# Graph attention heads: a fourth of ten source blocks taken from TensorE and ScalarE to VectorE, and the next head's rows turned and fetched earlier

## The reference, cut to what matters

```python
z = (x @ W).reshape(N, num_heads, head_dim)
el = jnp.sum(z * attn_l, axis=-1)
er = jnp.sum(z * attn_r, axis=-1)
e = jax.nn.leaky_relu(el[src] + er[dst], NEG_SLOPE)
m = jax.ops.segment_max(e, dst, num_segments=N)
ex = jnp.exp(e - m[dst])
denom = jax.ops.segment_sum(ex, dst, num_segments=N)
alpha = ex / denom[dst]
out = jax.ops.segment_sum(alpha[:, :, None] * z[src], dst, num_segments=N)
out = out + z + bias
```

## Time and profile before

| | |
|---|---|
| time, median of 3 runs | 3422.15 us (3420.96 to 3429.84) |
| profiled execution | 3426.71 us, its span 3425.0 us |
| mean granted TensorE clock | 0.916 of full |
| PE, PEld busy | 85%, 63% of the span |
| DVE, ACT, POOL busy | 56%, 33%, 4% |
| heads of g0, first to last exponent matmul and sums | about 360 to 831 us |
| heads of g1 | about 976 to 1446 us |

### The profile page before, as it was taken

One profiled execution on the slowest core, in us unless ns is written; L12 is line 12 of the kernel. 1 busy time (PEld: TensorE's weight loads), 2 busy tenths in 40 slices (PEclk: granted clock), 3 DMA queues, 4 the chain that ended last, 5 costly groups with the idle time before them and its releaser, 6 DMA issues.

```text
span 3425.0 us, 45464 instructions
## 1 busy us (share of the span) xinstructions
PE 2909.4 (85%) x14613; PEld 2142.6 (63%) x14614; DVE 1915.6 (56%) x3661; ACT 1137.0 (33%) x1827; POOL 132.9 (4%) x189
## 2 busy tenths in 40 slices
PE   6876699998949999896969679889995998896994
PEld 4543588887538888763657434468884565465772
DVE  7755899984679999557331134476641333532113
ACT  0111588875247777522014211121110220211110
POOL 0000000000000000000001110000000000000112
PEclk9888799999979999998979889979997999897995
DMA  1011111101011111100125542122213110023434
GB/s 67 0 35 42 45 47 61 49 37 50 2 67 46 45 55 48 50 0 25 58 78 190 189 126 72 45 75 82 74 30 135 44 40 21 32 79 112 165 136 146
DMA packets 80976, 231.30 MB, mean 68 GB/s; under 512 B 14037, under 2 KB 26783, under 8 KB 77985
## 3 DMA queue, kind: packets, MB, share of 16 engines
q1 hardware_dynamic: 58161, 166.83, 13.5%
q0 software_dynamic: 16304, 47.67, 4.7%
q10 hardware_dynamic: 6400, 15.36, 1.3%
HBM read 177.60 MB, written 54.94 MB: 68 GB/s over the span
## 4 chain that ended last, share of the span: by engine, by line
PE 39%; DVE 6%; DMA 5%; issue 2%; ACT 1%; POOL 0%; SPq 0%; ACTq 0%; DVEq 0%; POOLq 0%
PE psum L998 17%; PE psum L917 10%; PE psum L1123 4%; PE psum L1132 4%; DMA arena<-y_rows,arena 2%; DVE arena L1559 1%; DMA y_rows<-arena 1%; DMA arena<-xn_rows,arena 1%; PE psum L1071 1%; DMA arena<-raw 1%; DVE arena L1681 1%; DVE arena L1867 1%; PE psum L1105 1%; PE psum L1110 1%; PE psum L907 0%
## 5 line engine op out<-in xcount | busy, mean ns | idle before, releaser
L998 PE MATMUL psum<-arena 125*125 125x256 f32 (+3 forms) x2400 | 630.0, 422 | 46.2 <-DVE arena L1695 46.2
L917 PE MATMUL psum<-arena 128*125 128x384 f32 (+1 forms) x1840 | 662.6, 519 | 7.3 <-ACT arena L1235 7.3
L1028 PEld LDWEIGHTS psum<-arena 125*125 125x125 f32 x4800 | 579.7, 190 | 66.1 <-DVE arena L1692 16.0
L998 PEld LDWEIGHTS psum<-arena 125*125 125x125 f32 x2400 | 449.5, 189 | 215.7 <-DVE arena L1695 40.0
L1028 PE MATMUL psum<-arena 125*125 (+1 forms) x4800 | 566.0, 271 | 13.6 <-DVE arena L1692 13.6
L917 PEld LDWEIGHTS psum<-arena 128*125 128x125 f32 x1840 | 344.9, 190 | 298.7 <-issue 115.1
L1018 PE MATMUL psum<-arena,spread 126*125 126x313 f32 (+1 forms) x1344 | 438.4, 450 | 31.8 <-DMA arena<-r_rows 18.2
L1692 DVE SCALAR_TENSOR_TENSOR arena<-arena,edge_counts 125x625 f32<-125x625 f32 x480 | 383.1, 807 | 86.0 <-ACT arena L1320 85.3
L1625 DVE CUSTOM_DVE_ANT_0 arena<-arena,no_edge_bias 125x1250 bf16<-125x1250 f32 x270 | 393.3, 1457 | 32.8 <-DMA arena<-el_rows 27.3
L1307 ACT ACTIVATE arena<-arena,el 125x625 f32<-125x625 f32 x480 | 386.5, 806 | 38.2 <-DMA arena<-el_rows 38.2
L1320 ACT ACTIVATE arena<-psum,el 125x625 f32<-125x625 f32 x336 | 262.6, 781 | 204.9 <-PE psum L1018 185.1
(11 more groups left out here) (212 smaller groups left out, 2399.2 us busy)
## 6 DMA issues: line engine op xcount, KB each, us to landing
arena<-el_rows SPq DMA_DIRECT2D x51, 610.4 KB
arena<-in_L_ffn_W SPq DMA_DIRECT2D x16, 1152.0 KB, 9.2
y_rows<-arena SPq DMA_DIRECT2D x47, 384.0 KB, 2.4
arena<-r_rows SPq DMA_DIRECT2D x24, 610.4 KB
arena<-in_L_w SPq DMA_DIRECT2D x16, 768.0 KB, 6.3
arena<-in_L_gnn_W SPq DMA_DIRECT2D x4, 3072.0 KB, 14.6
raw<-arena POOLq DMA_DIRECT2D x40, 250.0 KB, 2.9
arena<-raw SPq DMA_DIRECT2D x10, 1000.0 KB
```

The lines of the kernel that those rows point to most:

```text
L917: ins = e.matmul(bank[0:P, 0:w], L.xt[u][:, k, :], L.w_sb[:, k, at:at + w], start=(k == 0), stop=(k == L.KT - 1))
L998: ins = e.matmul(banks[2 + 2 * (j % 2) + c][0:P, 0:w], Ph[half][:, s, d * P:(d + 1) * P], (L.zh[u] if L.spill else L.z)[:, s, at:at + w], ...
L1028: ins = e.matmul(banks[2 + half][0:P, d * 65:(d + 1) * 65], Ph[half][:, s, d * P:(d + 1) * P], L.z[:, s, h, :], start=(s == 0), stop=(s == ...
```

## The change

`ADD_AT` gets a fourth block, s = 5, so eight of a head's twenty blocks have their exponent from VectorE. The addition there is another one: instead of relu block + rb2 it is max(rb1 + el8, rb2), with a second broadcast row rb1. So the relu's of all eight blocks are dropped (`relu` returns), as are the exponent matmuls of blocks 5 and 15. SP writes all 20 rows of r_rows instead of 10 and loads rb1 and rb2. The load of the el row of head h + 2 moves from between the two halves' r2 rows to right behind the write, ahead of the wait for it. From head 1 on, the next head's rows are turned at block 4 and copied at block 5; head 0 keeps 11 and 12. ScalarE's code gets heads 0 and 1 out of its loop. Buffers in SBUF move to make room for rb1: the head buffers start at HEADS_AT, 40 columns above S_AT, and some buffers of the next layer's start move with them.

```diff
-ADD_AT = [3, 7, 9]
+ADD_AT = [3, 5, 7, 9]
...
+def rectified(j):
+
+    return j - of_vector(j)
...
-            rb_in=[16 * n * own for n in of_dma], relued=2 * T * heads * self.batched, t_ready=TURNS * heads * self.batched,
-            added=ADDS * heads * self.batched, rb2_in=[16 * n * self.batched for n in of],
+            rb_in=[16 * n * own for n in of_dma], relued=TURNS * heads * self.batched, t_ready=TURNS * heads * self.batched,
+            added=ADDS * heads * self.batched, rb2_in=[32 * n * self.batched for n in of],
...
+        ROWS_FROM = Z_AT + T * 12 * 65
+        HEADS_AT = ROWS_FROM + 2 * N
...
-            at = S_AT
+            at = HEADS_AT if L.batched else S_AT
...
+                L.rb1 = [carve(ROWS_FROM + u * N, P, N) for u in range(2)]
...
-        TURN_EARLY, ROWS_EARLY = 11, 12
+        TURN_EARLY, ROWS_EARLY = 4, 5
+        TURN_FIRST, ROWS_FIRST = 11, 12
...
-                e.dma_start(r_rows[h, T:2 * T, :], L.rt[u][T:2 * T, :]).then_inc(L.r_out[u], 16)
+                e.dma_start(r_rows[h, :, :], L.rt[u]).then_inc(L.r_out[u], 16)
+                if more:
+                    load_el(h + 2, u)
...
-                e.dma_start(L.rb2[u], over(r_rows[h, T:2 * T, :].rearrange("t p -> (t p)"))).then_inc(L.rb2_in[u], 16)
+                for rows, r in ((L.rb1, 0), (L.rb2, 1)):
+                    e.dma_start(rows[u], over(r_rows[h, r * T:(r + 1) * T, :].rearrange("t p -> (t p)"))).then_inc(L.rb2_in[u], 16)
...
-                    if half == 0 and more:
-                        load_el(h + 2, u)
...
-                    if j == TURN_EARLY and not last:
+                    if j == (TURN_FIRST if first else TURN_EARLY) and not last:
                         turn_r(h + 1, 1 - u)
...
+                if s in ADD_AT:
+                    return
...
-                    if j == ROWS_EARLY and not last:
+                    if j == (ROWS_FIRST if isinstance(h, int) and h == 0 else ROWS_EARLY) and not last:
                         rows(h + 1, 1 - u)
...
-                with e.Fori(0, L.H // 2 - 1) as i:
+                batched_head(0, 0, 0, False)
+                batched_head(1, 1, 0, False)
+                with e.Fori(1, L.H // 2 - 1) as i:
...
-                    e.wait_ge(L.rb2_in[u], L.since["rb2_in"][u] + 16 * (i + 1))
-                e.wait_ge(L.relued, L.since["relued"] + 2 * T * h + j + 1)
+                    e.wait_ge(L.rb2_in[u], L.since["rb2_in"][u] + 32 * (i + 1))
                 e.wait_ge(L.p_ready, L.since["p_ready"] + 2 * T * h + j + 1)
                 apart(e)
-                e.tensor_tensor(L.ex[j % 4], L.r2[half][0:P, s % 3, :], L.rb2[u][:, half * HALF:(half + 1) * HALF], ALU.add).then_inc(L.added, 1)
+                cols = slice(half * HALF, (half + 1) * HALF)
+                e.scalar_tensor_tensor(out=L.ex[j % 4], in0=L.rb1[u][:, cols], scalar=L.el8[:, s, bass.ds(h, 1)], in1=L.rb2[u][:, cols],
+                                       op0=ALU.add, op1=ALU.max).then_inc(L.added, 1)
```

More of the change, by code:

```diff
@@ L351, in graph_transformer @@
             else:
+                if L.inner is not None:
+                    at = HEADS_AT + 2 * N
                 L.xin = [carve(at + u * L.K, P, L.K) for u in range(2)]
@@ L356, in graph_transformer @@
                 at += 2 * L.K
-                L.xbias = carve(Z_AT + T * 12 * 65 if L.inner is not None else at, P, L.K)
+                L.xbias = carve(HEADS_AT + 2 * L.F if L.inner is not None else at, P, L.K)
                 at += L.K
@@ L364, in graph_transformer @@
                 L.sjunk = carve(at, P, 384).bitcast(BF16)
-            vectors_at = MADE_AT if L.spill else S_AT - 2 * L.F
+            vectors_at = MADE_AT if L.spill else HEADS_AT if L.inner is not None else S_AT - 2 * L.F
             L.al_b = [carve(vectors_at + u * L.F, P, L.F).rearrange("p (h d) -> p h d", h=L.H) for u in range(2)]
-            at = S_AT
+            at = HEADS_AT if L.batched else S_AT
             if L.H > 1:
@@ L643, in rows_of @@
                 def rows_of(h, u, i, more):
-                    e.wait_ge(L.relued, L.since["relued"] + 2 * T * (h - 1))
+                    e.wait_ge(L.relued, L.since["relued"] + TURNS * (h - 1))
                     apart(e)
@@ L1013, in exponents @@
                     e.wait_ge(L.r2_in[half], L.since["r2_in"][half] + 48 * (h + 1))
-                e.wait_ge(L.relued, L.since["relued"] + 2 * T * h + j + 1)
+                e.wait_ge(L.relued, L.since["relued"] + TURNS * h + rectified(j) + 1)
                 e.wait_ge(L.e_ready, L.since["e_ready"] + 2 * T * h + j + 1)
```

## The result

The changed kernel takes 3493.85 us (median of 4 runs, 3487.96 to 3497.49), the kernel before 3425.99 (4 runs, the three known ones and one more). The ratio is 1.019, 95% interval 1.017 to 1.022: slower by 1.9%, 68 us, where 37 were forecast. The profiled execution took 3494.81 us with a span of 3493.1, 68.1 us more than that of before.

A forecast was written before the change was run, and what follows sets the result against it. PE paced steady heads at 37.2 us, DVE close behind. Per layer 10.0 + 1.9 + 8.7 + 2.0 - 4.0 = +18.6 us, +37.2 for two, taking the median from 3422.2 to 3459.4, forecast 3460 us; range 3438 to 3484.

The forecast's parts named there:

- The direction and its first reason: Whole kernel slower, chance 0.90; in steady heads DVE becomes the limit, 38.2 us against PE's 37.2 before.
- the 0.2 us of disturbance: Steady heads: block 2 or 4 may reach DVE late, 0.2 us per head (bounds 0 and 0.5), making 38.4.
- The start: Start of each layer's heads: small r2 rows queue behind the el row and rb1 broadcasts, +8.7 us per layer.
- the small rows are not held up: Rival for the layer's start and h = 1: the 8.7 and 2.0 us vanish, result 3439 us; chance 0.10.
- Head 0: First head of each layer: two more additions and a dearer kind on DVE's path, +1.9 us per layer.
- Can DVE really run without waits?: Steady heads: PE idles about 3 us, then 3.4 us at half rate costs it 1.7: 36.8, under 38.2.
- PE's clock falls in every head for long: Rival for steady heads: half rate lasts some 17 us, PE needs 43.6 us; 3554 us in all; clock chance 0.10.
- case of every third head: Variant of the clock rival: the long half-rate stretch comes in every third head, some 3490 us in all.
- base of 35.1 us of PE work: PE per steady head: 37.2 us less 2.1 for the dropped exponent matmuls of blocks 5 and 15.
- the end of g0: Last max_end to last p_free in layer g0: 78.9 us, or 80.6 with 3.4 us at half rate; -4.0 taken.
- The start of h = 1: Second head: PE idles 4 us for late rows, likely falls to half rate; DVE waits, +2.0 us per layer.
- ACT's saved relu's and the earlier turn: Steady heads: eight relu's dropped at 0.8 us and loads moved to the fourth and fifth block gain nothing.

The follow-up runs named there:

- the first experiment: Changed kernel with the el row of head h + 2 loaded between the halves' small r2 rows again, as before the change: 3480.6 us, ratio 1.016.
- the first two experiments: Changed kernel with the el row's load back in its old place, 3480.6 us; changed kernel with small r2 rows first in heads 0 and 1, 3471.4 us.
- the last experiment: Kernel before, with four more unused VectorE additions of 625 columns per head in heads 1 to 9: 3492.5 us, ratio 1.020.
- experiment 8: Not a run's number: 8 counts waits in "the last experiment 8 of 9 waits"; that run is the kernel before with four more VectorE additions per head, 3492.5 us.

## Why the prediction was right or wrong, point by point

**The direction and its first reason held.** "So after the change DVE sets the pace, at 38.2 us against 37.2": a head without a fall is 38.27 us in both layers, without the 0.2 us of disturbance that were added to it. The addition costs the 0.78 us read from L1681, start to start:

```profile
478.12 0.86 DVE L1790 SCALAR_TENSOR_TENSOR arena<-arena,el 125x625 f32<-125x625 f32 x1
478.90 0.80 DVE L1708 SCALAR_TENSOR_TENSOR arena<-arena,edge_counts 125x625 f32<-125x625 f32 x1
```

The run without the scalar shows the 0.06 us that the row had over the old form. The Trainium skill's fixed part plus elements (VectorE: DVE Perf Modes, TRN2 errata) has no place for it; the measurement decides.

**The start held.** +9.1 and +8.9 us for the 8.7 worked out, and two runs with another order in the queue (DVE idle 22.0, 18.1, 7.3 us) show the cause. The rival "the small rows are not held up" is out. **Head 0** is exact.

**What failed: "Can DVE really run without waits?", in the price of the clock's fall.** The wait of PE was foreseen, at about 3 us; it is 2.1 to 2.2 us. The step then took the one case of the earlier trace rows, 3.4 us at half rate, as the size of every fall, and priced it at nothing, because 1.7 us fit under PE's slack. In the changed kernel the falls in steady heads last 6.8 us (head of 39.7 us), 10.2 (41.3) and 13.7 (42.9 to 43.0), in the first experiment 20.5 (46.2). The excess over 38.3 is half the length of the fall less PE's wait of 2.2 us: 6.8 / 2 - 2.2 = 1.2 for 1.5 measured, 13.7 / 2 - 2.2 = 4.7 for 4.6, 20.5 / 2 - 2.2 = 8.1 for 8.0. That is the mechanism of the rival "PE's clock falls in every head for long", which had 0.10. Its case of every third head is what came, and its 3490 us is near the 3494 measured, but in part by luck: it took every fall at 17 us and left the start of head 1 and the ends as they were forecast. Its base of 35.1 us of PE work was also low, since PE is busy for 36.07 us in head 2: with 35.1 a fall of 13.7 us would make a head of 42.0 us, with 36.07 one of 42.9, as measured. Heads 2 to 9 were +35.5 us instead of +18.8, and the end of g0, forecast with at most 3.4 us at half rate, had 13.7 and gave +1.6 instead of -4 us. Filler on PE takes all of this away, and load on DVE alone brings such falls about in the kernel before. The trace of before could not give the price: behind such a wait, with PE busy from then on, it has one fall per layer (413.1 us in g0, 1027.5 in g1), and both last 3.4 us. Its longer low stretches lie where PE waits again and again or has little to do.

**What failed second: "The start of h = 1", a term mis-sized.** PE's wait of 4 us was 6.3 and 6.7, and "likely falls to half rate" was priced at 3.2 us more of PE work. In g0 the clock was low for 34.1 us, 30 of them from the moment when PE could start: +14.3 us instead of +2.6, and +5.6 in g1, where the clock was low for 12 us from that moment on. The prediction saw only the late rows as the reason to wait. With the rows early PE waits 4.9 us at block 1 for DVE, which lags after head 0's twenty maxima. It did so before as well (2.94 us); two more additions in head 0 make it longer. With the small rows first it is 4.9 and 4.2 us with eight of the new additions, 2.8 and 3.4 with six.

**The end** came out as worked where the clock held: 78.9 us in g1.

**ACT's saved relu's and the earlier turn are worth nothing**, as said: with three blocks, where six blocks have no relu, a steady head takes the 37.2 us of before, and the earlier turn alone has a ratio of 1.000.

**What stays open.** Why a wait of the same 2.2 us is followed by a fall in one head and not in another, and what sets the length of a fall. What the runs show: in the changed kernel and the first two experiments 18 of 32 waits of 1.9 to 2.2 us had a fall behind them and none of 16 waits of about 1.0 us; with half the filler none of the waits of 1.0 to 1.1 us had one; in the last experiment 8 of 9 waits of 1.7 to 1.85 us had one.

## What to carry to other kernels

When a change makes another engine the limit, the loss is not the difference of the two periods alone: look where TensorE then waits. One fall of its clock in the trace does not give the length of the next: here 3.4 us before became 6.8 to 20.5 us, so such a term needs a wide range, or a run. If the wait can't be avoided, a few matmuls on constants in its place hold the clock, and a run with them tells the clock's share from the work's. In a queue, put the small transfer that an engine waits for ahead of the broadcasts; that alone made the kernel before 0.3% faster, and both versions that beat the kernel before have it.

## What the runs showed of the hardware that was not expected

- A fall of the granted clock to 0.50 after one wait of about 2 us lasted 3.4, 6.8, 10.2, 13.7, 17.1 or 20.5 us with PE busy without a gap meanwhile (20.50 of 20.50 us in the first experiment, 17.10 of 17.10 in the last).
- The falls keep a rhythm: in the first experiment g0 had them at 496.3, 619.1 and 742.0 us, 122.8 and 122.9 us apart, every third head, each 20.5 us long. In the changed kernel they lie 116 to 119 us apart, also every third head. In the last experiment they come in every second head, 78 to 85 us apart. The head behind a fall has a short wait: about 1.0 us in the changed kernel and the first experiment, 0.4 to 0.5 us in the last.
- Adding 2.1 us of unused matmuls per head made the kernel 36 us faster.
- A per-partition scalar from SBUF costs a VectorE instruction of 625 f32 columns 0.06 us (862 ns against 803).
